# Third scan: the spreads of u and delta on 32-row tiles of the TensorE array, two quarters at a time

## The chip, the cores and the metric

The kernel runs on one core of one Trainium2 chip. The time is device microseconds of that core, the median of three executions; lower is better. A profile is one execution of its own, with its own time.

## What is computed

The reference is a chain of four layers on a tensor of 8 x 64 x 32 x 32: window attention with an MLP, an anti-aliased activation, a selective scan of eight tokens (`scan2` in the kernel) and a selective scan over whole pictures (`scan3`, the third scan of the title), each with norms and projections around it. The change lies in scan3 alone. Cut to what matters:

```python
dt = softplus(dtr @ dt_w.T + dt_b)          # delta, one value per channel and token
A = -exp(A_log)
def step(h, inp):
    dt_t, B_t, C_t, x_t = inp
    dA = exp(dt_t[..., None] * A)           # decay, channels x 16 states
    h = dA * h + (dt_t * x_t)[..., None] * B_t[:, None, :]
    y = einsum('bds,bs->bd', h, C_t)
    return h, y
```

Here u stands for dt_t * x_t. The recurrence runs over 1024 tokens of each picture.

## The kernel before, in words

Channels stand on partitions and tokens on columns. A value of delta or u belongs to a channel, but the state has 16 values per channel, so delta and u have to be spread: each channel's row is copied onto 16 partitions. TensorE does this with a matmul by a matrix of zeros and ones (`selr`); selector 4q + g has its ones in rows 32q + 8g to 32q + 8g + 7 alone, that is inside quarter q of the 128 rows. So that float32 comes through exactly, each source is split into a high and a low part (`parts`, written by ScalarE and GpSimd), and a spread is two matmuls of 512 columns that add up in one PSUM bank.

The work is 64 steps. A step is one group of 8 channels out of each quarter, 512 tokens, and its four quarters q = 0 to 3 are handled one after the other with q % 2 picking one of two PSUM banks for delta (`ps_d`) and one of two for u (`ps_u`). Four steps share one block of 512 tokens; at each such group of four steps the new block's delta, u, B and C are prepared.

In one step of scan3 the engines do this:

- TensorE (in the order of `body`): spreads of u for q = 0, 1 (`inputs`), spread of delta q = 0 (`decays`), spread of B (`states(0)`), spread of delta q = 1, spreads of u q = 2, 3, spread of C (`states(1)`), spreads of delta q = 2, 3, and then `r_py`: four float32 matmuls on 128x32 tiles (tile positions (0, 32q)), which sum the products over the states. Once per group of four steps it also does L1481 (delta's projection) and L1485 (B and C).
- ScalarE: `r_decay` (L1595), the exponential of the spread delta, one instruction per quarter; copies of spread B and C out of PSUM (L1605); parts of the preparation.
- DVE (VectorE): `r_feed` (L1630), u times B, for two quarters; then `r_state` (L1643), the scan itself, for these two quarters; then the same for q = 2, 3. Once per group it folds y (L1659).
- POOL (GpSimd): `r_prod` (L1702), state times C, four per step, and once per group seven more operations: L1707 (low parts of B and C), L1675, L1677, L1680, L1685 (softplus), L1690 and L1693, and L1671.

Every engine runs its own program in order; semaphores tie them. The lags are written by hand: at step s TensorE spreads B and C of step s - 2, delta of s - 5, u of s - 6 and sums y of s - 7, while DVE and POOL work on s - 6. In each group's third step the spread of B waits for POOL's L1707 (`lo_bc`), which POOL does after the products of its second step. L1481 and L1485 write the same bank `ps_m` as the spreads of B and C, so states(0) waits for ScalarE's relu (L1562) or copy (L1568) in those steps. y waits for `multiplied`, the products of its step.

Of the kernel before, what the change touches and what calls it, by code (L numbers as in the profile page):

```python
# [16 lines left out]
P = 128  # L17
# [42 lines left out]
def wait(eng, sem, value):  # L60

    if isinstance(value, int) and value <= 0:
        return
    eng.wait_ge(sem, value)
# [767 lines left out]
UNROLL, PEEL = 8, 8  # L832
# [589 lines left out]
def scan3(nc, consts, xc, selr, ysel):  # L1422
# [4 lines left out]
    with ExitStack() as ctx:  # L1427
# [5 lines left out]
        parts = m.sb("r_parts", [P, 2, 3, 2, N], F32R)  # L1433
# [5 lines left out]
        ps_d, ps_u, feed = m.banks("r_pd", 2), m.banks("r_pu", 2), m.banks("r_feed", 2)  # L1439
# [6 lines left out]
        hi_d, hi_u, hi_bc, lo_d, lo_u, lo_bc = (m.sem("r_" + t) for t in ("hid", "hiu", "hibc", "lod", "lou", "lobc"))  # L1446
# [7 lines left out]
        DT, DU, BC = range(3)  # L1454
# [9 lines left out]
        def _(pe):  # L1464
# [5 lines left out]
            def spread(bank, sel, which, par):  # L1470
                for part in range(2):
                    mm = pe.matmul(bank[:], selr[:, sel * P:(sel + 1) * P], parts[:, par, which, part],  # L1472
                                   start=(part == 0), stop=(part == 1))
                return mm

            def body(s, u):
                par = u // 4
                gi = s - u % 4
# [8 lines left out]
                def decays(qs):  # L1487
                    p, v = s - LAG_D, u - LAG_D
                    if not live(p, STEPS):
                        return  # L1490
                    for q in qs:
                        if v % 4 == 0 and q == 0:
                            pe.wait_ge(lo_d, p + 4)
                        wait(pe, decayed, 4 * p + q - 1)
                        spread(ps_d[q % 2], 4 * q + v % 4, DT, v % UNROLL // 4).then_inc(d_ps, 1)

                def states(which):

# [15 lines left out]
                def inputs(qs, p, v):  # L1514
                    if not live(p, STEPS):
                        return
                    for q in qs:
                        if v % 4 == 0 and q == 0:
                            pe.wait_ge(lo_u, p + 4)
                        wait(pe, fed, 4 * p + q - 1)  # L1520
                        spread(ps_u[q % 2], 4 * q + v % 4, DU, v % UNROLL // 4).then_inc(u_rep, 1)

                inputs((0, 1), s - LAG_U, u - LAG_U)
                decays((0,))
                states(0)
                decays((1,))
                inputs((2, 3), s - LAG_U, u - LAG_U)
                states(1)
                decays((2,))
                decays((3,))  # L1530
                p, v = s - LAG_Y, u - LAG_Y
                if live(p, STEPS):
                    if v % 4 == 0:
# [11 lines left out]
        def _(act):  # L1545
# [6 lines left out]
            def body(s, u):  # L1552
# [35 lines left out]
                def decays(qs):  # L1588
                    p, v = s - LAG_D, u - LAG_D
                    if not live(p, STEPS):  # L1590
                        return
                    for q in qs:
                        act.wait_ge(d_ps, 4 * p + q + 1)
                        wait(act, scanned, 4 * (p - 2) + q + 1)
                        act.activation(decay[:, v % 2, q], ps_d[q % 2][:], ACT.Exp,  # L1595
                                       scale=aneg[:, v % 4:v % 4 + 1]).then_inc(decayed, 1)
# [20 lines left out]
        def _(dve):  # L1617
# [3 lines left out]
            def body(s, u):  # L1621
                p, v = s - LAG_U, u - LAG_U
                if live(p, STEPS):
                    b, g, lc = v % 2, v % 4, v % UNROLL // 4
                    def inflow(q):
                        dve.wait_ge(u_rep, 4 * p + q + 1)
                        if g == 0:
                            dve.wait_ge(b_copied, p + q + 1)
                        wait(dve, scanned, 4 * p + q - 1)
                        dve.tensor_tensor(feed[q % 2][:], ps_u[q % 2][:], bs[:, lc, q], ALU.mult).then_inc(fed, 1)  # L1630
# [165 lines left out]
```

## Time and profile before

| | us |
|---|---|
| median of 3 runs | 2071.08 |
| lowest and highest | 2064.47, 2071.54 |
| the profiled execution, its own time | 2069.05 |
| its span | 2067.3 |
| scan3 in it, first matmul to last product | about 1432 to 1961 |

The span is what the profiler saw between the first and the last instruction; 1.75 us lie around it. Busy shares are of the whole span. PE is TensorE's matmuls, PEld its weight loads, which overlap matmuls. The granted clock of TensorE is 1.00 at 2.4 GHz and 0.50 at 1.2 GHz. A bracket at the end of a timeline row tells how long the engine had been idle before it, and for whom it waited; an x8 at its form means eight instructions merged into one row.

### The profile page before, as it was taken

Reading aid. Unit: us, or ns where it says so; the run is one execution under the profiler, and the core shown is the slowest. Engines: PE = TensorE matmul, PEld = TensorE weight load, DVE = VectorE, ACT = ScalarE, POOL = GpSimd, SP = SyncE. Lnnn points to the kernel's source line nnn. Section 1 sums busy time; section 2 is a strip of 40 time slices with the busy share of each in tenths; the row PEclk is TensorE's granted clock in tenths of the full one; section 3 lists DMA queues with packets and bytes.
Section 4 is the critical chain, followed back from the end, with each engine's and each line's share of the span. In section 5 each row is a group of like instructions: output and inputs, shape, how many; then the busy total and the mean of one; then the engine's idle time right before and its main releaser. Section 6 shows DMA issues by size and latency. Waiting matters only on the chain. (4 is left out here: it accounts for less than half of the span.)

```text
span 2067.3 us, 30819 instructions
## 1 busy us (share of the span) xinstructions
PE 1656.4 (80%) x9846; PEld 982.2 (48%) x9846; DVE 1602.7 (78%) x1580; ACT 1122.0 (54%) x1825; POOL 1391.9 (67%) x897
## 2 busy tenths in 40 slices
PE   5888787996777777787877777667788898888787
PEld 2555445883444444444444444325454555555323
DVE  3788655555899999999999999642699999999954
ACT  3444484344555555555555555365666666666355
POOL 1666401003999999999999999501799999999701
PEclk8999998997999999999999999888899999999888
DMA  4000000000000000000000000000000000000001
GB/s 130 2 0 0 1 0 1 1 1 0 1 1 1 0 0 0 0 0 0 0 0 0 0 0 0 18 0 1 1 1 0 0 0 0 0 0 0 1 12 41
DMA packets 5004, 11.04 MB, mean 5 GB/s; under 512 B 1744, under 2 KB 2768, under 8 KB 4688
## 3 DMA queue, kind: packets, MB, share of 16 engines
q1 hardware_dynamic: 4944, 10.29, 1.7%
q8 instruction: 32, 0.52, 0.1%
q14 instruction: 28, 0.23, 0.0%
HBM read 8.19 MB, written 2.10 MB: 5 GB/s over the span
## 5 line engine op out<-in xcount | busy, mean ns | idle before, releaser
L1157 POOL TENSOR_TENSOR s_ahead<-s_ahead,s_back 128x1024 f32<-128x1024 f32 x128 | 305.2, 2384 | 44.3 <-DVE s_back L1140 41.3
L1702 POOL TENSOR_TENSOR r_prod<-r_state,r_cs 128x512 f32<-128x512 f32 x256 | 323.5, 1304 | 16.3 <-DVE r_state L1643 15.9
L1194 POOL TENSOR_TENSOR s_prod<-s_ahead,s_cs 128x1024 f32<-128x1024 f32 x128 | 304.7, 2381 | 6.8 <-POOL s_ahead L1157 4.3
L1137 DVE TENSOR_TENSOR_SCAN s_ahead<-s_fore,s_pfeed 128x1024 f32<-128x1024 f32 x128 | 292.4, 2284 | 6.7 <-ACT s_fore L1056 1.6
L1140 DVE TENSOR_TENSOR_SCAN s_back<-s_aft,s_pfeed 128x1024 f32<-128x1024 f32 x128 | 289.4, 2261 | 0.0
L1056 ACT ACTIVATE s_fore<-s_pd,s_aneg 128x896 f32<-128x896 f32 x128 | 129.8, 1014 | 265.0 <-PE s_pd L936 265.0
L936 PE MATMUL s_pu<-s_partsu,selr 128*128 128x512 f32 x512 | 174.0, 464 | 100.0 <-DVE s_pfeed L1120 99.8
L1630 DVE TENSOR_TENSOR r_feed<-r_pu,r_bs 128x512 f32<-128x512 f32 x256 | 164.5, 686 | 65.0 <-PE r_pu L1472 65.0
L1595 ACT ACTIVATE r_decay<-r_pd,r_aneg 128x512 f32<-128x512 f32 x256 | 168.2, 685 | 24.4 <-PE r_pd L1472 24.1
L936 PEld LDWEIGHTS s_pu<-s_partsu,selr 128*128 128x128 f32 x512 | 94.1, 197 | 175.1 <-DVE s_pfeed L1120 124.0
L1120 DVE TENSOR_TENSOR s_pfeed<-s_pu,s_bs 128x1024 f32<-128x1024 f32 x128 | 157.8, 1233 | 18.6 <-PE s_pu L936 5.5
L1472 PE MATMUL r_pu<-r_parts,selr 128*128 128x512 f32 x512 | 162.7, 440 | 5.7 <-DVE r_feed L1630 5.7
L1643 DVE TENSOR_TENSOR_SCAN r_state<-r_decay,r_carry,r_feed 128x512 f32<-128x512 f32 x128 | 156.2, 1261 | 0.0
L1472 PE MATMUL r_pd<-r_parts,selr 128*128 128x512 f32 x512 | 155.4, 407 | 0.0
L936 PE MATMUL s_pd<-s_partsd,selr 128*128 128x512 f32 x512 | 150.1, 418 | 0.0
L994 PE MATMUL s_py<-s_prod,ysel 128*32 128x128 f32 x2048 | 142.5, 408 | 8.7 <-POOL s_prod L1194 8.7
L1643 DVE TENSOR_TENSOR_SCAN r_state<-r_decay,r_feed 128x512 f32<-128x512 f32 x128 | 148.5, 1201 | 0.0
L1472 PE MATMUL r_pm<-r_parts,selr 128*128 128x512 f32 x256 | 93.0, 446 | 59.3 <-POOL r_parts L1707 45.9
L1061 ACT ACTIVATE s_aft<-s_pd,s_aneg 128x896 f32<-128x896 f32 x128 | 129.9, 1015 | 0.0
L1472 PEld LDWEIGHTS r_pu<-r_parts,selr 128*128 128x128 f32 x512 | 95.1, 195 | 72.0 <-issue 39.2
L936 PEld LDWEIGHTS s_pd<-s_partsd,selr 128*128 128x128 f32 x512 | 105.0, 205 | 25.0
L650 POOL TENSOR_TENSOR logit<-logit,top 128x512 f32<-128x512 f32 x64 | 66.7, 1042 | 70.6 <-DVE top L621 70.6
(249 smaller groups left out, 3339.7 us busy)
## 6 DMA issues: line engine op xcount, KB each, us to landing
x_act<-in_x_dram SPq DMA_DIRECT2D x8, 256.0 KB, 5.3
out_dram<-x_act SPq DMA_DIRECT2D x16, 128.0 KB, 2.3
k_scan<-in_pack_scan_dram SPq DMA_DIRECT2D x1, 1600.0 KB, 10.2
k_fir<-in_pack_fir_dram SPq DMA_DIRECT2D x1, 1600.0 KB, 13.6
k_ln<-in_pack_ln_dram SPq DMA_DIRECT2D x3, 131.0 KB, 2.7
k_mlp<-in_pack_mlp_dram SPq DMA_DIRECT2D x2, 194.0 KB, 4.8
k_l<-in_pack_l_dram SPq DMA_DIRECT2D x1, 386.0 KB, 6.7
k_attn<-in_pack_attn_dram SPq DMA_DIRECT2D x1, 358.0 KB, 6.8
```

Source lines behind the costliest of these rows:

```text
L936: mm = pe.matmul(bank, selr[:, sel * P:(sel + 1) * P], parts[:, part], start=(part == 0), stop=(part == 1))
L994: mm = pe.matmul(ps_y[quad * 32:(quad + 1) * 32, j * NPX:(j + 1) * NPX], ysel[:, (2 * odd + g) * 32:(2 * odd + g + 1) * 32], terms[:, 2 * ...
L1120: dve.tensor_tensor(feed[:], ps_u[:], bs[:, buf].rearrange("p i n -> p (i n)"), ALU.mult).then_inc(fed, 1)
L1137: dve.tensor_tensor_scan(ahead[:, b], f, feed[:], 0.0, ALU.mult, ALU.add).then_inc(ahead_done, 1)
L1140: dve.tensor_tensor_scan(back[:, b, ::-1], a[:, ::-1], feed[:, ::-1], 0.0, ALU.mult, ALU.add).then_inc(back_done, 1)
L1157: pool.tensor_tensor(ahead[:, b], ahead[:, b], back[:, b], ALU.add).then_inc(summed, 1)
L1194: pool.tensor_tensor(prod[:, b], ahead[:, b], cs[:, buf].rearrange("p i n -> p (i n)"), ALU.mult).then_inc(prod_done, 1)
L1472: mm = pe.matmul(bank[:], selr[:, sel * P:(sel + 1) * P], parts[:, par, which, part], start=(part == 0), stop=(part == 1))
L1595: act.activation(decay[:, v % 2, q], ps_d[q % 2][:], ACT.Exp, scale=aneg[:, v % 4:v % 4 + 1]).then_inc(decayed, 1)
L1630: dve.tensor_tensor(feed[q % 2][:], ps_u[q % 2][:], bs[:, lc, q], ALU.mult).then_inc(fed, 1)
L1643: dve.tensor_tensor_scan(state[:, b, q], decay[:, b, q], feed[q % 2][:], start, ALU.mult, ALU.add).then_inc(scanned, 1)
L1702: pool.tensor_tensor(prod[:, v % 2, q], state[:, v % 2, q], cs[:, v % UNROLL // 4, q], ALU.mult).then_inc(multiplied, 1)
```

## The change

For u and for delta, the two quarters of a pair (0 and 1, or 2 and 3) are now spread by one helper, `pair`. Each of its matmuls takes only the 32 rows of its quarter, of `selr` and of `parts`, with tile position (32q, 0), so it uses a 32 x 128 tile of the array. The order inside is high part of the one quarter, high part of the other, low part of the one, low part of the other. The semaphore is raised by 2 after the last matmul; ScalarE and DVE wait for the whole pair, and TensorE waits until both banks of the pair have been read. The order of the step on TensorE becomes u 0 and 1, delta 0 and 1, B, u 2 and 3, C, delta 2 and 3, y. The spreads of B and C still use the old `spread` on the whole array. The number of matmuls and of their columns stays.

```diff
--- before.py
+++ after.py
@@ -1473,6 +1473,15 @@
                                    start=(part == 0), stop=(part == 1))
                 return mm
 
+            def pair(banks, sel, qs, which, par):
+                for part in range(2):
+                    for q in qs:
+                        rows = slice(32 * q, 32 * q + 32)
+                        mm = pe.matmul(banks[q % 2][:], selr[rows, (4 * q + sel) * P:(4 * q + sel + 1) * P],
+                                       parts[rows, par, which, part], start=(part == 0), stop=(part == 1),
+                                       tile_position=(32 * q, 0))
+                return mm
+
             def body(s, u):
                 par = u // 4
                 gi = s - u % 4
@@ -1488,11 +1497,10 @@
                     p, v = s - LAG_D, u - LAG_D
                     if not live(p, STEPS):
                         return
-                    for q in qs:
-                        if v % 4 == 0 and q == 0:
-                            pe.wait_ge(lo_d, p + 4)
-                        wait(pe, decayed, 4 * p + q - 1)
-                        spread(ps_d[q % 2], 4 * q + v % 4, DT, v % UNROLL // 4).then_inc(d_ps, 1)
+                    if v % 4 == 0 and qs[0] == 0:
+                        pe.wait_ge(lo_d, p + 4)
+                    wait(pe, decayed, 4 * p + qs[1] - 1)
+                    pair(ps_d, v % 4, qs, DT, v % UNROLL // 4).then_inc(d_ps, 2)
 
                 def states(which):
 
@@ -1514,20 +1522,17 @@
                 def inputs(qs, p, v):
                     if not live(p, STEPS):
                         return
-                    for q in qs:
-                        if v % 4 == 0 and q == 0:
-                            pe.wait_ge(lo_u, p + 4)
-                        wait(pe, fed, 4 * p + q - 1)
-                        spread(ps_u[q % 2], 4 * q + v % 4, DU, v % UNROLL // 4).then_inc(u_rep, 1)
+                    if v % 4 == 0 and qs[0] == 0:
+                        pe.wait_ge(lo_u, p + 4)
+                    wait(pe, fed, 4 * p + qs[1] - 1)
+                    pair(ps_u, v % 4, qs, DU, v % UNROLL // 4).then_inc(u_rep, 2)
 
                 inputs((0, 1), s - LAG_U, u - LAG_U)
-                decays((0,))
+                decays((0, 1))
                 states(0)
-                decays((1,))
                 inputs((2, 3), s - LAG_U, u - LAG_U)
                 states(1)
-                decays((2,))
-                decays((3,))
+                decays((2, 3))
                 p, v = s - LAG_Y, u - LAG_Y
                 if live(p, STEPS):
                     if v % 4 == 0:
@@ -1590,7 +1595,7 @@
                     if not live(p, STEPS):
                         return
                     for q in qs:
-                        act.wait_ge(d_ps, 4 * p + q + 1)
+                        act.wait_ge(d_ps, 4 * p + q // 2 * 2 + 2)
                         wait(act, scanned, 4 * (p - 2) + q + 1)
                         act.activation(decay[:, v % 2, q], ps_d[q % 2][:], ACT.Exp,
                                        scale=aneg[:, v % 4:v % 4 + 1]).then_inc(decayed, 1)
@@ -1623,7 +1628,7 @@
                 if live(p, STEPS):
                     b, g, lc = v % 2, v % 4, v % UNROLL // 4
                     def inflow(q):
-                        dve.wait_ge(u_rep, 4 * p + q + 1)
+                        dve.wait_ge(u_rep, 4 * p + q // 2 * 2 + 2)
                         if g == 0:
                             dve.wait_ge(b_copied, p + q + 1)
                         wait(dve, scanned, 4 * p + q - 1)
```

## Rows read from the trace of the kernel before

**Rows 1.** The page of before: busy shares of the engines over the whole span.

```profile
PE 1656.4 (80%) x9846; PEld 982.2 (48%) x9846; DVE 1602.7 (78%) x1580; ACT 1122.0 (54%) x1825; POOL 1391.9 (67%) x897
```

**Rows 2.** The page of before: TensorE and its clock in 40 slices (tenths).

```profile
PE   5888787996777777787877777667788898888787
...
PEclk8999998997999999999999999888899999999888
```

**Rows 3.** Windows: busy us and clock between starts of L1675 (one to five groups).

```profile
core 0: us, PE busy (x) PEld busy (x) DVE busy (x) ACT busy (x) POOL busy (x), PEclk, DMA share, GB/s
1463.20:1497.06 33.86, 28.63 (x120) 17.55 (x120) 30.26 (x36) 23.29 (x44) 30.38 (x26) 1.00 0.00 1
1497.06:1651.39 154.33, 131.36 (x580) 78.23 (x580) 144.47 (x166) 96.31 (x173) 151.56 (x121) 1.00 0.00 0
1528.18:1558.86 30.68, 26.30 (x116) 15.69 (x116) 28.43 (x34) 19.65 (x37) 30.27 (x25) 1.00 0.00 0
1651.39:1746.08 94.69, 82.65 (x348) 50.59 (x348) 86.05 (x100) 59.05 (x107) 91.00 (x73) 0.95 0.00 0
1746.08:1776.98 30.90, 26.26 (x116) 15.62 (x116) 29.23 (x34) 19.00 (x33) 30.32 (x25) 0.98 0.00 0
1776.98:1872.82 95.84, 83.57 (x348) 51.38 (x348) 85.96 (x100) 59.08 (x107) 91.07 (x74) 0.93 0.00 0
1872.82:1903.71 30.89, 26.23 (x116) 15.62 (x116) 29.20 (x34) 19.00 (x33) 30.31 (x25) 1.00 0.00 0
```

**Rows 4.** Waits of POOL, then of DVE, from 1497.06 to 1903.71 us.

```profile
POOL r_prod L1702 <- DVE r_state L1643: 5.8, 9, 0.9
...
DVE r_feed L1630 <- PE r_pu L1472: 30.9, 36, 2.4
```

**Rows 5.** Timeline of PE: one step that waits for nothing (start us, us).

```profile
1719.18 1.06 PE L1537 MATMUL r_py<-r_prod,ysel 128*32 128x512 f32 x8
...
1722.61 1.09 PE L1472 MATMUL r_pu<-r_parts,selr 128*128 128x512 f32 x4
...
1723.55 0.63 PE L1472 MATMUL r_pm<-r_parts,selr 128*128 128x512 f32 x2
...
1725.04 1.07 PE L1537 MATMUL r_py<-r_prod,ysel 128*32 128x512 f32 x8
```

**Rows 6.** Timeline: POOL's L1707 and what follows, clock at its upper level.

```profile
1526.95 1.26 POOL L1707 TENSOR_TENSOR r_parts<-r_bcf,r_parts 128x512 fp32r<-128x512 f32 x1
...
1528.27 0.30 PEld L1472 LDWEIGHTS r_pm<-r_parts,selr 128*128 128x128 f32 x2 [3.58 <-POOL r_parts L1707]
...
1530.12 1.32 DVE L1630 TENSOR_TENSOR r_feed<-r_pu,r_bs 128x512 f32<-128x512 f32 x2 [1.12 <-PE r_pu L1472]
```

**Rows 7.** Timeline: the same place with the clock at its lower level.

```profile
1775.75 1.27 POOL L1707 TENSOR_TENSOR r_parts<-r_bcf,r_parts 128x512 fp32r<-128x512 f32 x1
...
1777.08 1.22 PE L1472 MATMUL r_pm<-r_parts,selr 128*128 128x512 f32 x2 [3.16 <-POOL r_parts L1707]
...
1780.20 0.70 DVE L1630 TENSOR_TENSOR r_feed<-r_pu,r_bs 128x512 f32<-128x512 f32 x1 [2.39 <-PE r_pu L1472]
```

**Rows 8.** Timeline of PE, then DVE: from ScalarE's relu to the next feed.

```profile
1793.55 0.72 PE L1472 MATMUL r_pm<-r_parts,selr 128*128 128x512 f32 x2 [1.11 <-ACT r_relu L1562]
...
1799.97 1.30 DVE L1630 TENSOR_TENSOR r_feed<-r_pu,r_bs 128x512 f32<-128x512 f32 x2 [1.20 <-PE r_pu L1472]
```

**Rows 9.** Timeline of POOL, then DVE: the last step of an undisturbed group.

```profile
1578.40 10.22 POOL L1702 TENSOR_TENSOR r_prod<-r_state,r_cs 128x512 f32<-128x512 f32 x8
...
1580.02 1.30 DVE L1630 TENSOR_TENSOR r_feed<-r_pu,r_bs 128x512 f32<-128x512 f32 x2 [0.32 <-PE r_pu L1472]
...
1584.76 2.44 DVE L1643 TENSOR_TENSOR_SCAN r_state<-r_decay,r_carry,r_feed 128x512 f32<-128x512 f32 x2
```

**Rows 10.** Timeline: POOL in the first group, then DVE near the end.

```profile
1489.95 2.54 POOL L1702 TENSOR_TENSOR r_prod<-r_state,r_cs 128x512 f32<-128x512 f32 x2 [1.39 <-DVE r_state L1643]
...
1923.80 1.30 DVE L1630 TENSOR_TENSOR r_feed<-r_pu,r_bs 128x512 f32<-128x512 f32 x2 [0.29 <-PE r_pu L1472]
```

## The prediction

> **What bounds the kernel now.** The change touches scan3 alone, so I asked first which engine sets its pace. The busy shares of the whole span name TensorE first (80%) [rows 1], but they mix four layers. So I cut scan3 into its groups of four steps, at the starts of POOL's L1675, and read windows [rows 3]: POOL is busy 30.3 us in every group, and a group lasts 30.7 to some 32 us. POOL's nearest rival DVE has 28.4 us in groups whose scans start from zero and 29.2 in those that start from a carry; TensorE about 26 to 28. POOL is the bound. The gaps between its instructions are hand-overs inside its own chain (L1677 to L1685), so I take the shortest group, 30.68 us, as the floor of a group. No edit here touches a POOL instruction.
>
> The 13 whole groups from 1497.06 to 1903.71 take 406.65 us. The floor is 13 x 30.68 = 398.84, so 7.8 us lie above it, and POOL's waits say what most of them are: 5.8 us for DVE's scans [rows 4]. DVE in turn waited 30.9 us for spreads of u, and for nearly nothing else [rows 4]. Most of that is harmless; what counts is the part by which DVE comes late to the last step of a group. In [rows 3] the seven groups with the clock at 0.98 to 1.00 (five in one window of 154.33, then 30.90 and 30.89) average 30.87 us. The six with it at 0.95 and 0.93 (two windows of 94.69 and 95.84 us, three groups each) average 31.76. So nearly all that can be won is in groups where TensorE's clock has dropped.
>
> Three places carry DVE's waits:
>
> (a) Behind L1707. The spread of B waits for it, and everything of TensorE's queue waits behind that, u 2 and 3 included. From L1707's end to the feed it takes 1.91 us at the upper clock [rows 6] and 3.18 at the lower [rows 7]. Before the first of these feeds lie six matmuls of 512 columns (B, delta 1, u 2).
>
> (b) From ScalarE's relu to the next step's feed: 6.42 us [rows 8], in which TensorE does 16 such matmuls, y and L1485. DVE waits 1.20 us at its end. This comes in the groups that start from zero.
>
> (c) Behind y, which waits for POOL: y of step p - 2 stands ahead of u 0 and 1 of step p. It leaves POOL almost nothing: the last two products of the eight start at about 1578.40 + 10.22 - 2.5 = 1586.1, and the first of the two scans from 1584.76 ends at about 1586.0 [rows 9].
>
> **The change, part by part.** Unhindered, TensorE issues a full-array matmul every 0.235 us (four in 0.94: 1722.61 to 1723.55), and a step from y to y takes 5.86 us [rows 5].
>
> Pairing. Sixteen of the 20 spread matmuls of a step go on 32-row tiles. The trace has no row tiles; its nearest rows are y's 128x32 column tiles: eight instructions in 1.06 us [rows 5], four tiles side by side. So the cost of four paired matmuls lies between 0.94 us (one after the other) and 0.47 (two by two), and not below, since a column needs its slot in each of two passes. I take 0.47: the neighbour along the other axis shares fully, the two quarters write different banks, and the loads don't stand in the way, since two loads take 0.30 us together [rows 6], so the second comes about 0.11 after the first. That saves 4 x 0.47 = 1.9 us of TensorE's step.
>
> Changes of tile shape. Before, a step has two: into y and out of it. Now B and C stand between paired spreads, which adds four. Price from [rows 5]: 5.86 - 20 x 0.235 - 4 x 0.235 (y's four passes) = 0.22 for two, so 0.11 each. The upper bound is an array that empties and then loads: a lone matmul takes 0.63 - 0.235 = 0.40 us instead of 0.235, and the loads' 0.19 are no longer hidden, 0.35 in all. Taken: 0.11, the only shape change the trace shows; 0.44 a step, with 1.4 as the far end. TensorE's free-running step falls from 5.9 to about 4.4 us.
>
> The Trainium skill speaks against this part: TensorEngine Tiling (Array Packing), section Key Properties, says that changing the tiling mode, not just the tile, drains TensorE. The trace shows 0.11 us for it; by a full drain the sum would go to its far end.
>
> Coarser waits. The feed of q = 0 now waits for the low part of q = 1: about 0.11 us later in (c) (the offset of a load). u 2 and 3 wait for both feeds; DVE then has 2.3 to 2.4 us of scans [rows 9] to cover a pair of 0.47 plus some 0.4 of latency: nothing. ScalarE's first exponential likewise. Delta 2 and 3 wait for ScalarE's exponential of q = 1, which stands behind the copy of B: about 0.3 us of TensorE's step, hidden under POOL.
>
> What it is worth at each place. (a): six slots become four, one shape change more: 1.91 to about 1.55, and at the lower clock, with slots twice as long, 3.18 to about 2.5. (b): 16 slots become 10, three shape changes more, and the C spread now waits for ScalarE's copy of B (about 0.3): 6 x 0.235 - 0.33 - 0.3 = 0.8 of the 1.20 us. (c): 0.1 later, against a margin of 0.1.
>
> The clock works against it. TensorE stood idle 3.16 us before the lower-clock case [rows 7]; it will stand about 1 us longer. So I let all 13 groups have their low stretch. Such a group takes 31.76 now; less 0.7 for (a), and in every second one 0.8 for (b), but not under the floor and with 0.1 for (c), it comes to about 31.0. 13 x 31.0 = 403.0: a gain of 3.6 us. With the clock as now, 4.3. Taken: 4.
>
> First group: 33.86 us, 3.2 above the floor [rows 3], with waits for DVE such as 1.39 us [rows 10]. It has (b) once, and the first feed comes 0.3 earlier: gain 1.1.
>
> End: from the feed at 1923.80 [rows 10] DVE runs without a pause to its last scan; that feed is released through y by POOL, as in (c). Gain 0.
>
> **Sum:** 2069.05 (the profiled execution's own time, 2067.3 of span and 1.75 around it) - 4.0 - 1.1 = 2064.0 us. That execution lies 2.0 below the median of 2071.08, but inside the runs (2064.47 to 2071.54), and the mean of these and it is 2069.0; so I forecast 2064 as it stands.
>
> **The rivals.**
>
> *TensorE gets out of the way entirely.* POOL runs at its floor: -7.8 for the 13 groups and -2.3 for the first one's waits: 2059.0. For it: TensorE's 1.4 us less a step. Against it: (c) is a loop through POOL, which a faster TensorE hardly shortens.
>
> *No overlap, or loads that block* (the other side). If the pairs run one after the other, TensorE's step grows to 5.86 + 0.44 = 6.3 us, at the far end 7.3, and each feed of q = 0 comes 0.47 later than now. In (c) only 0.1 of that is covered, so 0.37 in each of 14 groups; (a) and (b) grow by 0.1 to 0.35 for each shape change, 0.4 a group. 14 x 0.77 + 0.5 at the end = 11: 2080. With the far end of the shape change TensorE has 4 x 7.3 + 1.1 + some 3 of waits = 33.3 us a group and becomes the bound: 2100. It decides from the point where four paired matmuls take over about 0.6 us. For it: nothing in the trace shows row tiles; against it: y. One rule of the Trainium skill would bring it about: TensorE: Matmul & The Clock Gate, Part 3, The mechanism, says that a weight load overlaps matmuls in flight only if its row group differs, and the low part's load has the row group of the high part's matmul. The trace disagrees for the full array, where loads of about 0.19 us hide inside a pitch of 0.235. The same page's measured speedup for four row tiles, 3.07, speaks for the overlap.
>
> *The clock.* TensorE's busy share of a group falls from 0.86 to about 0.67 (26.3 - 7.5 + 1.8 of 31). In the four slices from 1292 to 1499 us, where TensorE is busy 6 to 7 tenths, the clock is at 8 tenths; in others with 7 tenths it is at 9 [rows 2]. At 1.2 GHz throughout, its step would take some 9 us, more than POOL's 7.7. If every group lost, on top of today's time, what the three from 1776.98 lose to the floor (95.84 / 3 - 30.68 = 1.3 at a clock of 0.93) [rows 3], that is 13 x 1.3 = 17: 2086. It decides from a granted clock of about 0.85 in a group.
>
> *It doesn't matter at all:* DVE's lateness comes from chains I take for covered, and the time stays: 2069.
>
> **How the numbers follow.** Forecast 2064 (2060 to 2068): 0.48. Floor reached, 2059: 0.14. No change, 2069: 0.12. No overlap or blocking loads, 2080: 0.18. Clock, 2086: 0.08. About 0.5%, 10 us, is what a measurement of this kernel can tell from no change. Faster by more, under 2060.7 from the median: most of the floor case, a little of the forecast's spread: 0.17. Slower, over 2081.4: half of the no-overlap case, the clock case, and some spread of runs: 0.20. The same: 0.63. The range leaves out the far ends (a drained array, half of the clock case) and below reaches past the floor by the spread of runs: 2055 to 2083.
>
> **What would show it.** In the profile after: four paired matmuls of u in about 0.5 us of TensorE's time (over 0.8 would mean no overlap); TensorE's step around 4.4 us between y and y; its wait for L1707 longer by 1 us, the feed behind it at 1.6 or 2.5 us; POOL's waits for DVE under 3 us; groups of 30.7 to 31.1. A group under 30.6 would mean that POOL's floor was read wrongly, and one over 32 with POOL waiting for DVE that the pairs or the clock cost more than they give.

## The result and the profile after

The changed kernel takes 2119.75 us (median of four, 2117.50 to 2165.84) against 2067.77 us before (2063.75 to 2071.54): the ratio is 1.0248, with a 95% interval from 1.0225 to 1.0270. It is slower by 52 us, where I had forecast 2064 us: 7 us under the median then shown, and 5 under the profiled execution. Its profiled execution took 2121.61 us, with a span of 2119.8. Some kernels with row tiles have a second, longer time, 48 to 60 us above the first and at a lower mean clock of the span (2165.84 at 0.856 here, the others at 0.873 to 0.878); ratios leave it out, and what brings it about is open.

The page after: busy shares, then TensorE and its clock in 40 slices, to be read against [rows 1, 2].

```profile
PE 1698.2 (80%) x9846; PEld 907.7 (43%) x9846; DVE 1605.3 (76%) x1580; ACT 1130.4 (53%) x1825; POOL 1389.5 (66%) x897
...
PE   5888778996778887888887786586988878888877
...
PEclk8999999998999999999999999795658687777589
```

As many matmuls as before, POOL and DVE as busy as before, and TensorE busy for 42 us more, though each pair was meant to halve its work. The clock row points at a reason: up to slice 27 it is that of before within a tenth, and in the slices of scan3 behind it is at 5 to 8 tenths where it had been at 8 and 9. Windows show it as in [rows 3]: the first group, the 13 groups that follow, and the end up to the last product; then the two halves of one group. POOL's L1675 is L1680 here.

```profile
core 0: us, PE busy (x) PEld busy (x) DVE busy (x) ACT busy (x) POOL busy (x), PEclk, DMA share, GB/s
1463.17:1505.40 42.23, 39.14 (x122) 15.40 (x122) 28.95 (x34) 24.21 (x44) 30.18 (x25) 0.50 0.00 1
1505.40:1951.24 445.84, 374.94 (x1508) 145.34 (x1508) 378.49 (x432) 258.92 (x454) 391.72 (x314) 0.74 0.00 0
1951.24:2014.92 63.68, 53.98 (x192) 20.85 (x192) 55.01 (x63) 23.73 (x41) 48.90 (x40) 0.50 0.00 1
1694.20:1711.30 17.10, 12.56 (x68) 4.92 (x66) 15.66 (x19) 12.49 (x23) 13.68 (x12) 1.00 0.00 0
1711.30:1728.40 17.10, 16.12 (x50) 6.05 (x50) 13.35 (x15) 7.29 (x12) 16.62 (x14) 0.51 0.00 0
```

Where the time lies: the first group takes 42.23 us (33.86 before), the 13 groups 445.84 (406.65), the end 63.68 (57.39; that window of before runs from 1903.71 to 1961.10). That is 8.4 + 39.2 + 6.3 = 53.9 us, and the rest of the span gives 1.4 back. A group lasts 34.3 us on average, and POOL is busy 30.1 us in it, as before: it is not slower, it waits. The last two rows show how a group goes: 17.1 us at 2.4 GHz, 17.1 us at 1.2 GHz. At the lower level TensorE is busy 94% of the time, at the upper one 73% (12.56 of 17.10).

Some of the longest waits of three engines in the 13 groups (total us, times, longest), for [rows 4]:

```profile
DVE r_feed L1635 <- PE r_pu L1480: 59.7, 39, 3.5
...
PEld r_pm L1472 <- ACT r_bs L1610: 41.5, 52, 1.4
PE r_pm L1472 <- POOL r_parts L1712: 41.2, 13, 3.7
...
POOL r_prod L1707 <- DVE r_state L1648: 34.2, 39, 3.1
```

POOL waits 34.2 us for DVE's scans, up from 5.8, DVE 59.7 us for spreads of u, up from 30.9. The chain runs from TensorE to DVE to POOL. Now the timeline of PE through the low half:

```profile
1712.28 1.22 PE L1472 MATMUL r_pm<-r_parts,selr 128*128 128x512 f32 x2 [3.00 <-POOL r_parts L1712]
1713.43 1.22 PE L1480 MATMUL r_pu<-r_parts,selr 32*128 32x512 f32 x4
1714.57 1.22 PE L1472 MATMUL r_pm<-r_parts,selr 128*128 128x512 f32 x2
...
1716.87 1.94 PE L1542 MATMUL r_py<-r_prod,ysel 128*32 128x512 f32 x8
1718.74 1.22 PE L1480 MATMUL r_pu<-r_parts,selr 32*128 32x512 f32 x4
1719.76 1.05 PE L1480 MATMUL r_pd<-r_parts,selr 32*128 32x512 f32 x4
1720.74 1.22 PE L1472 MATMUL r_pm<-r_parts,selr 128*128 128x512 f32 x2
1721.89 1.22 PE L1480 MATMUL r_pu<-r_parts,selr 32*128 32x512 f32 x4
1723.04 1.22 PE L1472 MATMUL r_pm<-r_parts,selr 128*128 128x512 f32 x2
1724.19 1.22 PE L1480 MATMUL r_pd<-r_parts,selr 32*128 32x512 f32 x4
1725.34 1.94 PE L1542 MATMUL r_py<-r_prod,ysel 128*32 128x512 f32 x8
```

Three things stand in it. **The pairing works:** four paired matmuls on 32-row tiles last as long as two on the whole array (1.22 each), and the eight of u and delta take 1720.74 - 1718.74 = 2.00 us. **The shape changes are dear** (a change is the time between whole-array and 32-row matmuls beyond their slots, a slot being the step from one 512-column matmul to the next): two whole-array matmuls and a change take 1721.89 - 1720.74 = 1.15, and eight paired ones and a change 2.00; with x for a slot and c for a change, 2x + c = 1.15 and 4x + c = 2.00 give x = 0.425 and c = 0.30 us. **The step:** from y to y 8.47 us without a wait, where POOL's products and preparation want about 7.6. At this clock TensorE is the bound. (An estimate for the old step at this clock, from this slot and the 1.87 us from y to the next matmul: 20 x 0.425 + 1.87 = 10.4 us. So at this clock, too, the new step is shorter than the old one; what costs is how long the clock stays there.)

At the upper clock, PE then DVE, out of two places of the trace:

```profile
1705.72 0.73 PE L1472 MATMUL r_pm<-r_parts,selr 128*128 128x512 f32 x2 [0.92 <-ACT r_bs L1610]
...
1706.38 0.73 PE L1480 MATMUL r_pd<-r_parts,selr 32*128 32x512 f32 x4
...
1707.04 1.06 PE L1542 MATMUL r_py<-r_prod,ysel 128*32 128x512 f32 x8
...
1729.60 1.30 DVE L1635 TENSOR_TENSOR r_feed<-r_pu,r_bs 128x512 f32<-128x512 f32 x2 [2.32 <-PE r_pu L1480]
```

Two whole-array slots and a change take 0.66 us; less 2 x 0.235 from [rows 5] that is 0.19 for a change. Four paired matmuls and a change take 0.66 as well, so the four take 0.47. And TensorE had waited 0.92 us for ScalarE's copy of B ahead of C, which the shorter queue no longer covers. The last row is what a low half leaves: a feed that comes 2.32 us late though the clock is up again.

### The profile page after: what moved, and what is told of

Read it like the earlier page. It is cut to its first block and busy times, and to the rows that moved or that the text cites. A ratio compares the mean times of both kernels' runs of the same rounds, so it can differ in the third digit from the quotient of the medians.

```text
span 2119.8 us, 30644 instructions
## 1 busy us (share of the span) xinstructions
PE 1698.2 (80%) x9846; PEld 907.7 (43%) x9846; DVE 1605.3 (76%) x1580; ACT 1130.4 (53%) x1825; POOL 1389.5 (66%) x897
## 5 line engine op out<-in xcount | busy, mean ns | idle before, releaser
L1707 POOL TENSOR_TENSOR r_prod<-r_state,r_cs 128x512 f32<-128x512 f32 x256 | 320.5, 1280 | 55.0 <-DVE r_state L1648 52.3
L1472 PE MATMUL r_pm<-r_parts,selr 128*128 128x512 f32 x256 | 131.6, 607 | 73.2 <-POOL r_parts L1712 47.7
L1480 PE MATMUL r_pu<-r_parts,selr 32*128 32x512 f32 x512 | 125.4, 576 | 12.7 <-DVE r_feed L1635 12.5
L1480 PE MATMUL r_pd<-r_parts,selr 32*128 32x512 f32 x512 | 117.6, 545 | 2.4 <-ACT r_decay L1600 2.4
L1472 PEld LDWEIGHTS r_pm<-r_parts,selr 128*128 128x128 f32 x256 | 53.9, 262 | 144.5 <-POOL r_parts L1712 55.7
```

Of the source, the lines that this page charges most:

```text
L1480: mm = pe.matmul(banks[q % 2][:], selr[rows, (4 * q + sel) * P:(4 * q + sel + 1) * P], parts[rows, par, which, part], start=(part == 0), s ...
L1707: pool.tensor_tensor(prod[:, v % 2, q], state[:, v % 2, q], cs[:, v % UNROLL // 4, q], ALU.mult).then_inc(multiplied, 1)
```

## The experiments

The theory after this reading: the 32-row form lowers the granted clock, and most of the loss is that. The rivals: the new order and the coarser waits; the added changes of shape; the saved microseconds of work, that is, a less busy TensorE in whatever form. Below, "groups" is the mean of the whole groups after the first, "clock" the granted one and "busy" TensorE's share in them.

**The order and the waits alone, whole array.** The changed kernel with this edit to `pair`:

```diff
-                        rows = slice(32 * q, 32 * q + 32)
-                        mm = pe.matmul(banks[q % 2][:], selr[rows, (4 * q + sel) * P:(4 * q + sel + 1) * P],
-                                       parts[rows, par, which, part], start=(part == 0), stop=(part == 1),
-                                       tile_position=(32 * q, 0))
+                        mm = pe.matmul(banks[q % 2][:], selr[:, (4 * q + sel) * P:(4 * q + sel + 1) * P],
+                                       parts[:, par, which, part], start=(part == 0), stop=(part == 1))
```

> The changed kernel with the new order and the waits for whole pairs, but with matmuls on the whole array again. Clock theory (the shorter and narrower work lets the clock fall, and the fallen clock makes DVE late): TensorE is as busy as before, the granted clock of scan3 is about 0.96, and the time is that of before, 0 to +5 us. Rival (the order and the coarser waits cost it): most of the +52 us stays, over +25 us, with the clock near 0.95.

2079.48 us, ratio 1.0062 [1.0039, 1.0085]; groups 31.7 us, clock 0.96, busy 0.88. So all but 0.6% of the 2.5% hangs on the form of the matmuls. In this profile the first group takes 36.91 us at a clock of 0.94, 3 us more than before.

**The tile form alone, old order and old waits.** The kernel before, whose spreads of u and delta call this in place of `spread`:

```diff
+            def tile(bank, sel, which, par):
+                rows = slice(32 * (sel // 4), 32 * (sel // 4) + 32)
+                for part in range(2):
+                    mm = pe.matmul(bank[:], selr[rows, sel * P:(sel + 1) * P], parts[rows, par, which, part],
+                                   start=(part == 0), stop=(part == 1), tile_position=(32 * (sel // 4), 0))
+                return mm
```

> The kernel before with only the form of the spreads of u and delta changed: each quarter's two matmuls take a 32-row tile, in the old order and with the old waits. Two of one quarter can't overlap; quarters that stand next to each other in the queue can. Clock theory: the clock of scan3 falls to 0.8 or less although TensorE has nearly as much to do as before, and the time is +25 to +80 us. Rival (it is the new order that brings the low clock, by leaving TensorE idle in long pieces): the clock stays above 0.9 and the time within +15 us.

One run took 2116.67 us and three 2165.04 to 2167.37. The profile is of one of the three (2166.8): clock 0.66 over 12 groups of 37.6 us. The run to compare is the one of 2116.67, with a mean clock of the span of 0.880, against the changed kernel's 2117.50 to 2121.61 with 0.873 to 0.878. So the form brings the low clock without the new order, the high-then-low issue or the coarse waits, and in the one run that can be compared, which has no profile, it brings the whole loss. Neighbouring quarters overlap in this order too: four matmuls of u take 1.22 us at the lower clock, as in the changed kernel.

**B and C on row tiles too**, so that no shape changes are added. The changed kernel with this for states:

```diff
-                    spread(ps_m, 16 + 2 * (v % 4) + which, BC, v % UNROLL // 4).then_inc((b_rep, c_rep)[which], 1)
+                    rows = slice(32 * (v % 4), 32 * (v % 4) + 32)
+                    for part in range(2):
+                        mm = pe.matmul(ps_m[:], selr[rows, (16 + 2 * (v % 4) + which) * P:(17 + 2 * (v % 4) + which) * P],
+                                       parts[rows, v % UNROLL // 4, BC, part], start=(part == 0), stop=(part == 1),
+                                       tile_position=(32 * (v % 4), 0))
+                    mm.then_inc((b_rep, c_rep)[which], 1)
```

> The changed kernel with the spreads of B and C on 32-row tiles as well, so that the four extra changes of tile shape in a step are gone; everything else stays. Clock theory: no gain, +45 to +70 us against before, granted clock of scan3 at 0.75 or less. Rival (the changes of shape cost it, some 0.3 us each, 16 in a group): the time falls by 15 us or more against the changed kernel, to +35 or less.

2113.14 us, 1.0222 [1.0204, 1.0241]: 0.3% back of 2.5. Groups 34.1 us, and the clock lower still, 0.60. The four added shape changes are not the main cause; with fewer whole-array matmuls in the step the clock fell further, so the 0.3% may be what is left of two opposite effects, and is not the price of the changes.

**Whole-array fillers in the changed kernel.** Matmuls of a constant into the bank of B, overwritten by the spread after them: 12 in the step that waits for POOL's low parts of B and C, ahead of that wait and behind a wait for `bcf_done`, 4 ahead of B in the others and 2 ahead of each C.

```diff
+            def filler(n):
+                for _ in range(n):
+                    pe.matmul(ps_m[:], selr[:, 0:P], selr[:, 0:N], start=True, stop=True)
...
-                        if v % 4 == 0:
-                            pe.wait_ge(lo_bc, p + 4)
...
+                        if v % 4 == 0:
+                            pe.wait_ge(bcf_done, p + 4)
+                        filler(12 if v % 4 == 0 else 4)
+                        if v % 4 == 0:
+                            pe.wait_ge(lo_bc, p + 4)
                     else:
                         pe.wait_ge(b_copied, p + 1)
+                        filler(2)
```

> The changed kernel with added matmuls on the whole array whose result is overwritten: 4 (12 where POOL's low parts of B are awaited, ahead of that wait) before each spread of B and 2 before each spread of C. They add about 1.4 us of work to each of TensorE's steps at the upper clock. Clock theory: the clock of scan3 is over 0.95 and the time comes back to that of before or better, -10 to +8 us. Rival (shape changes or coarser waits): the time stays at +50 us or grows by the added work.

2083.66 us, 1.0077 [1.0053, 1.0100]. More work on TensorE and 35 us less time ((1.0248 - 1.0077) x 2068). Windows over the first group, the 13 groups and the end; columns as in [rows 3], here and for the next two kernels:

```profile
1462.97:1505.68 42.71, 39.44 (x168) 20.56 (x168) 30.60 (x36) 24.13 (x44) 30.40 (x25) 0.84 0.00 1
1505.68:1917.44 411.76, 386.90 (x1924) 188.26 (x1924) 374.87 (x430) 261.12 (x453) 392.55 (x314) 0.99 0.00 0
1917.44:1974.76 57.32, 42.11 (x212) 18.25 (x212) 54.52 (x63) 23.28 (x41) 48.94 (x40) 0.80 0.00 1
```

The groups give 34.1 us back and the end 6.4 (it is at the 57.39 of before); the first group stays as long as in the changed kernel, though its clock rose from 0.50 to 0.84.

**Busy on tiles.** Is it the idle time that the fillers fill, or their form? The changed kernel with each pair issued twice over, on its tiles (the second time gives the same values):

```diff
-                for part in range(2):
+                for part in (0, 1, 0, 1):
```

> The changed kernel with the matmuls of every pair issued twice, the first set overwritten: TensorE is about as long at work as before the change, but on 32-row tiles. If being at work for a shorter time is what lets the clock fall, the clock is over 0.9 and the time within +20 us of before. If the work on 32-row tiles does not hold the clock however long it lasts, the clock stays at 0.75 or less and the time rises above the changed kernel's, +60 to +130 us.

2295.84 us, 1.1116 [1.1083, 1.1149]. The profile is of its slowest execution (2355.2); the span's clock was 0.802 in it and 0.822 to 0.829 in the four others, against 0.939 to 0.944 with whole-array fillers. The window is of 11 groups.

```profile
1519.32:2068.10 548.78, 536.75 (x1992) 259.01 (x1990) 325.91 (x367) 222.15 (x384) 333.04 (x265) 0.55 0.00 0
```

TensorE is busy 98% and has a clock of 0.55; with whole-array fillers it was busy 94% and had 0.99. The busy share alone does not account for the clock.

**64-row tiles, old order.** The kernel before with `tile` as above, but on halves of the rows:

```diff
-                rows = slice(32 * (sel // 4), 32 * (sel // 4) + 32)
+                rows = slice(64 * (sel // 8), 64 * (sel // 8) + 64)
...
-                                   start=(part == 0), stop=(part == 1), tile_position=(32 * (sel // 4), 0))
+                                   start=(part == 0), stop=(part == 1), tile_position=(64 * (sel // 8), 0))
```

> As the run with tiles in the old order (+48 or +97 us, clock 0.66 over 13 groups), but each spread of u and delta takes a 64-row tile; changes of shape, order and waits are the same. If the number of rows at work decides about the clock, it lies well above 0.66, over 0.8, and the time at +5 to +35 us. If every tiled form is treated alike, or the changes of shape are the cost, it is as slow as with 32 rows, +45 us or more.

2215.51 us, 1.0706 [1.0688, 1.0723]. It is the second branch of the expectation that came, for the clock and for the time. The window is of 11 groups.

```profile
1502.53:1956.55 454.02, 430.20 (x1276) 201.47 (x1276) 326.39 (x364) 225.46 (x383) 332.75 (x265) 0.66 0.00 0
```

Clock 0.66 with TensorE busy 95%. Quarters 0 and 1 lie in the same half here, and so do 2 and 3, and neighbours do not overlap: at the upper clock the four matmuls of delta 2 and 3 and the change after them take 1.10 us (1615.13 to 1616.23). So there is more work than with 32 rows at a clock as low, and a group takes 41.3 us.

**The coarse waits of u alone**, whole array, order of before:

```diff
-                    for q in qs:
-                        if v % 4 == 0 and q == 0:
-                            pe.wait_ge(lo_u, p + 4)
-                        wait(pe, fed, 4 * p + q - 1)
-                        spread(ps_u[q % 2], 4 * q + v % 4, DU, v % UNROLL // 4).then_inc(u_rep, 1)
+                    if v % 4 == 0 and qs[0] == 0:
+                        pe.wait_ge(lo_u, p + 4)
+                    wait(pe, fed, 4 * p + qs[1] - 1)
+                    for part in range(2):
+                        for q in qs:
+                            mm = pe.matmul(ps_u[q % 2][:], selr[:, (4 * q + v % 4) * P:(4 * q + v % 4 + 1) * P],
+                                           parts[:, v % UNROLL // 4, DU, part], start=(part == 0), stop=(part == 1))
+                    mm.then_inc(u_rep, 2)
...
-                        dve.wait_ge(u_rep, 4 * p + q + 1)
+                        dve.wait_ge(u_rep, 4 * p + q // 2 * 2 + 2)
```

> The kernel before with the old order and the whole array, but the spreads of u issued two quarters together (high parts, then low parts) with one wait and one release for the pair. The new order with all coarse waits cost +12.8 us. If the coarser waits for u are most of that, +6 to +12 us here (the feed of quarter 0 then waits for two matmuls more, 0.47 us, 14 groups); if the order and delta's part are, 0 to +5 us.

2082.72 us, 1.0061 [1.0045, 1.0078], groups 32.1 us, clock 0.96: as much as the order-and-waits run lost. The mechanism is in the timeline, PE then DVE, at the place of [rows 9]:

```profile
1577.77 1.06 PE L1540 MATMUL r_py<-r_prod,ysel 128*32 128x512 f32 x8 [0.38 <-POOL r_prod L1705]
...
1580.94 1.30 DVE L1633 TENSOR_TENSOR r_feed<-r_pu,r_bs 128x512 f32<-128x512 f32 x2 [0.31 <-PE r_pu L1522]
```

From y to the feed 3.17 us; before it was 2.71 (1577.31 to 1580.02): 0.46 more, the two slots of q = 1, in a loop through POOL that had 0.1 to spare. POOL's waits for DVE rise to 16.2 us. On the tiles, where q = 1 runs beside q = 0, the same stretch of the filler kernel, from its y at 1674.70, is this:

```profile
1675.70 1.12 PE L1494 MATMUL r_pm<-y_inner,r_wdtb 128*128 x2
1676.75 0.74 PE L1480 MATMUL r_pu<-r_parts,selr 32*128 32x512 f32 x4
1677.61 1.30 DVE L1643 TENSOR_TENSOR r_feed<-r_pu,r_bs 128x512 f32<-128x512 f32 x2 [1.01 <-PE r_pu L1480]
```

It takes 2.91 us, 0.20 more than before. That is not the coarse wait: L1494, on the whole array, now stands ahead of a 32-row pair, and a change of shape is 0.19. From the pair's start to the feed it is 0.86 us, and 0.86 too in the last kernel of this section, which waits for each quarter by itself (1647.50 to 1648.36).

**The new order alone**, whole array, old waits: the kernel before with

```diff
-                decays((0,))
+                decays((0, 1))
                 states(0)
-                decays((1,))
                 inputs((2, 3), s - LAG_U, u - LAG_U)
                 states(1)
-                decays((2,))
-                decays((3,))
+                decays((2, 3))
```

> The kernel before with the new order of the step (delta of quarters 0 and 1 ahead of B, delta 2 and 3 last), the whole array, and the old waits for single quarters. If the order is most of the 12.8 us of the earlier run, +6 to +12 us; if the coarser waits are, 0 to +5 us.

2065.09 us, 0.9985 [0.9973, 0.9996] over 12 runs; groups 30.9, clock 0.98. POOL waits 0.9 us for DVE in all (5.8 before). The order is the one part of the change that helps, by 3 us, just clear of the noise.

**Fillers in the kernel before**, 12 of them at the wait for the low parts of B and C, none elsewhere (`filler` and the moved waits as above):

```diff
+                        filler(12 if v % 4 == 0 else 0)
+                        if v % 4 == 0:
+                            pe.wait_ge(lo_bc, p + 4)
```

> The kernel before with 12 matmuls on the whole array, whose result is overwritten, ahead of the wait for POOL's low parts of B, once in four steps (2.8 us of work in a wait of 3.2 us). If the low stretches of the clock in six of thirteen groups are what costs the kernel before its time over POOL's floor, the clock of scan3 is 1.00 in nearly all groups and the time falls by 3 to 8 us. Rival (the fillers hold up the spread of B and what stands behind it): 0 to +8 us.

2065.59 us, 0.9981 [0.9971, 0.9992]; groups 30.9 us, clock 1.00. **New order and these fillers together:**

> The kernel before (whole array, old waits) with the new order of the step and the 12 fillers ahead of the wait for POOL's low parts of B. Each alone gave -3 to -4 us, and each by taking DVE's lateness out of the same place, the end of a group. If they take the same microseconds, -3 to -6 us together; if they add up, -7 to -9 us. Groups of 30.8 us, clock 1.00.

2066.45 us, 0.9987 [0.9973, 1.0001]; groups 30.9, clock 1.00. The two gains don't add. In each, POOL's waits for DVE are all but gone (5.8 us before), so it seems that both take away the same waits, and what is left is POOL. In windows over 13 groups, fillers first, the order second:

```profile
1499.04:1900.35 401.31, 377.19 (x1664) 232.77 (x1664) 374.94 (x430) 251.18 (x453) 394.37 (x314) 1.00 0.00 0
```

```profile
1497.32:1898.79 401.47, 346.63 (x1508) 207.13 (x1508) 375.43 (x430) 253.07 (x453) 393.60 (x313) 0.98 0.00 0
```

**Fillers in the changed kernel at that wait alone** (12, and none elsewhere):

> The changed kernel with the 12 whole-array fillers ahead of the wait for POOL's low parts of B alone, and none elsewhere (the run with fillers everywhere gave a clock of 0.99 over 13 groups and +16 us). If the clock falls because of the long wait, it stays above 0.95 and the time is +5 to +18 us. If it falls because the rest of the step, too, has little whole-array work, the clock lies between 0.75 and 0.9 and the time at +25 to +45 us.

2128.91 us, 1.0288 [1.0273, 1.0302]: slower than the changed kernel without them, against what I expected. PE and POOL in the timeline:

```profile
1709.73 3.01 PE L1487 MATMUL r_pm<-selr 128*128 128x512 f32 x12
1709.88 1.29 POOL L1720 TENSOR_TENSOR r_parts<-r_bcf,r_parts 128x512 fp32r<-128x512 f32 x1
...
1712.58 0.63 PE L1472 MATMUL r_pm<-r_parts,selr 128*128 128x512 f32 x2
```

The low parts are there at 1711.17, but B starts at 1712.58: after a low half TensorE comes to this place late, and the fillers no longer lie in idle time. A filler pays where the queue waits anyway, and there it didn't. The clock rose to 0.79 only, inside the range that I had put beside the second branch (too little whole-array work in the rest of the step); the time went past both of my ranges. In this trace the clock falls again at 1722 us, with no wait of TensorE over 1.49 us since 1712.58. So the long wait is not the only place where it falls.

**The best I could make of the tiles**: the kernel with fillers, and the waits fine again. `pair` waits for and releases each quarter by itself, and ScalarE and DVE wait as before:

```diff
+                        if part == 0:
+                            wait(pe, free, 4 * p + q - 1)
...
+                        if part == 1:
+                            mm.then_inc(done, 1)
...
-                        act.wait_ge(d_ps, 4 * p + q // 2 * 2 + 2)
+                        act.wait_ge(d_ps, 4 * p + q + 1)
...
-                        dve.wait_ge(u_rep, 4 * p + q // 2 * 2 + 2)
+                        dve.wait_ge(u_rep, 4 * p + q + 1)
```

> The changed kernel with the fillers everywhere (clock held, +16 us) and single waits and releases for each quarter instead of one for the pair. With the whole array the coarse wait for u cost 0.47 us a feed and +13 us. On tiles a pair takes 0.47 us in all, so if the wait costs only the offset of the second quarter, 0.1 to 0.2 us, the time falls by no more than 5 us, to +11 to +16. If the coarse wait is what keeps the +16, it falls by 8 us or more.

2079.31 us, 1.0050 [1.0031, 1.0069]; groups 31.4, clock 1.00, first group 38.8 us at 0.96. It is still slower than before. Its profile is of the fastest of its four runs (2075.07). What remains in it is in the first group (4.9 us over before), where the fillers' own time can lie on the path, and in the groups (408.06 against 406.65 us, where the three kernels with POOL's waits taken away have 401). TensorE's loads for u wait 0.7 us for DVE's feeds in the groups, against 6.2 with the coarse waits: what the fine ones save is the wait for banks.

The loss of 0.0248 x 2068 = 51 us, by these runs: holding the clock gives 35 back, and more if the fillers cost time themselves. Of the 16 left (0.0077 x 2068), the two profiles (of before and with fillers) put 8.9 in the first group (42.71 against 33.86) and 5.1 in the 13 groups. Finer waits take away about half of that in the profiles, 3.9 and 3.7 us; by the ratios it is 6, but their intervals overlap. What remains is 10 over the kernel before, and the order hides a gain of 3 in it. Candidates are the changes of shape (0.19 us each at the upper clock, 0.19 of them in the loop through POOL), the fillers themselves, and round trips to ScalarE that lost their cover. I have no run that parts these.

## Why the prediction was wrong, point by point

**The bound, and where the time could be won: right.** POOL's busy time per group didn't move (30.1 against 30.3 us), and no kernel's groups average less than 30.86 us, which the three kernels that take away POOL's waits reach (the floor was put at 30.68). The prize was 8 to 10 us at most.

**The pairs: right.** 0.47 us for four, the lower of my bounds, as four took the time of two on the whole array (1.22 us at the lower clock, 0.73 at the upper). In the pair at 1708.03 all four weight loads, two for each row group, are done 0.30 us after its start, with its first matmuls still running. The Trainium skill's rule in TensorE: Matmul & The Clock Gate, Part 3, The mechanism, that a load overlaps matmuls in flight only if its row group differs, is not what this trace shows.

**The changes of shape: mis-sized.** Taken 0.11, measured 0.19 us at the upper clock and 0.30 at the lower, six a step instead of two, and one more that I left out, behind L1481 or L1485, in the two steps of a group that have them. The 0.11 came from the changes into and out of y, whose tiles use all 128 rows, and shared a remainder of 0.22 between two; 0.35 was my far end, so it is inside the bounds. The difference, 0.08 us for each of six changes in four steps, is some 2 us of TensorE's time a group, and at a held clock TensorE is not the bound. The Trainium skill's sentence in TensorEngine Tiling (Array Packing), Key Properties, that a change of the tiling mode drains TensorE, is nearer to this trace than my choice was: a lone matmul takes 0.40 us instead of 0.235, and 0.19 us is about that difference.

**The coarse waits: right for the tiles, by the rows that can be compared.** I took 0.11 us for the feed of q = 0 in (c), and from pair to feed the coarse wait cost nothing (0.86 us either way). The feed still came 0.20 later, by the change of shape that I had left out, in the place where I had said that nothing was to spare. On the whole array the same waits cost 0.46 us a feed and 12.6 us of time. For u 2 and 3 and delta 2 and 3 I took the wait for both banks as free; the fine waits took 5.5 us of waiting for feeds from TensorE, and no run shows what that alone was worth.

**The step of TensorE: 4.4 us was foretold.** At the upper clock the trace's stretches add up to 1.00 (y) + 1.13 (u and delta, 4 x 0.235 + 0.19) + 4 x 0.66 = 4.8 us; it never runs so, since ScalarE's copies hold it up. The one place where I let that cost anything had 0.3 us; the wait for the copy of B is 0.92 in the row above, and TensorE's loads wait 41.5 us for it over the 13 groups, against 8.8 before.

**The clock: the step that failed.** The sum let all 13 groups have a low stretch and priced such a group as one of before, at 31.76 us, to come down to 31.0 by the change's gains; measured were 34.3 us, at a clock of 0.74. I had the mechanism among the rivals, at a chance of 0.08 and a price of 17 us; the fillers give 35 back. Three errors in it:
- I measured the danger by TensorE's busy share, 0.86 falling to 0.67, and set it against slices of the profile with that share and a clock of 0.8. At the upper clock it did fall, to 0.73 (12.56 / 17.10); over the 13 groups it is 0.84 (374.94 / 445.84), as in [rows 3] (131.36 / 154.33 = 0.85), because the same work lasts longer at the lower clock, and the clock is 0.74 where [rows 3] had 1.00. And 98% busy on tiles had 0.55. The slices that I compared with hold no row tiles, and their busy share did not carry over.
- I priced it by what the groups of before lose at a clock of 0.93. But in those groups the low stretches were short. At 1.2 GHz a step takes 8.47 us (I had written "some 9", and the condition with it), more than POOL's, so TensorE becomes the bound for half of each group, and the chain TensorE, DVE, POOL carries it into the upper half (2.32 us at 1729.60).
- I took the wait for L1707 to be what drops the clock, and let it grow by 1 us. It hardly grew (PE waited 41.2 us in the 13 groups, against 39.8 before; 3.00 at 1712.28, 3.16 in [rows 7]), and the clock stayed low for 17.1 us. In the kernel before it was back after about 7, as windows of 2 us behind [rows 7] show (columns as in [rows 3]); in between TensorE was as busy as in the changed kernel:

```profile
1775.00:1777.00 2.00, 0.00 (x0) 0.00 (x0) 2.00 (x3) 0.00 (x0) 2.00 (x3) 0.71 0.00 0
1777.00:1779.00 2.00, 1.92 (x5) 1.54 (x6) 0.81 (x1) 0.60 (x1) 1.85 (x3) 0.50 0.00 0
1779.00:1781.00 2.00, 2.00 (x6) 1.60 (x5) 0.70 (x1) 0.69 (x1) 1.87 (x2) 0.50 0.00 0
1781.00:1783.00 2.00, 2.00 (x6) 1.32 (x4) 1.95 (x3) 1.00 (x2) 1.87 (x3) 0.59 0.00 0
1783.00:1785.00 2.00, 2.00 (x13) 0.97 (x13) 1.67 (x3) 1.61 (x4) 2.00 (x2) 1.00 0.00 0
```

This is the longest of the six low stretches in the 13 groups of before; the other five were half as long. In the changed kernel all 13 groups have one, of 17 us or more. So the clock falls twice as often and takes some 2.5 to 5 times as long to come back: the tiles delay its return more than they bring about its fall.

For the first group I took a gain of 1.1 us and for the end 0; they lost 8.4 and 6.3, at a clock of 0.50 in both. The end's loss is the clock's: the fillers gave it back whole. The first group's is not settled. In the whole-array run of the order and the waits it took 36.91 us at a clock of 0.94, and with the order alone 33.85, so some 3 of the 8.4 are what the coarse waits cost there; with fillers it took 42.71 us at a clock of 0.84.

**The signs I had named** did their work: "one over 32 with POOL waiting for DVE" is what the profile shows, and both causes I had written beside it, pairs or clock, were then parted by the fillers and the whole-array run. The sign for the wait for L1707, longer by 1 us, did not come, and a step of 4.4 us was never seen.

## What to carry to other kernels

Row tiles halve TensorE's slots, but in a kernel whose bound is another engine the saved slots are worth next to nothing, while the clock they ran at can be lost: read the granted clock of the stretch first, and work out the step at 1.2 GHz against the step of the engine that bounds. If that step is the longer one, the tile form is a risk that the saving has to pay for, the more so the longer the clock stays low. When two quarters are handed over together, look at what the first one then waits for: two slots of the other on the whole array (0.46 us a feed), nothing where both run side by side. And look at the order of the queue by itself, since here the plain reordering, on the whole array, was the part that gained, if only 3 us.

## What was unexpected of the hardware

- The form of the matmuls went with the clock, and how busy TensorE was did not: 0.55 at 98% busy (32-row tiles twice, in the slowest execution), 0.66 at 95% (64-row tiles), 0.74 at 84% (the change), 0.60 at 87% (B and C on tiles too), against 0.98 at 86% (new order, whole array) and 0.99 at 94% (the change with whole-array fillers).
- The Trainium skill, TensorE: Matmul & The Clock Gate, Part 1, ties the clock to how busy TensorE has been. If busy is read as the share in these rows, this case's runs disagree for row tiles: 98% busy, and 0.55.
- A change between the whole array and 32-row tiles costs 0.19 us at 2.4 GHz and 0.30 at 1.2 GHz.
- Row tiles overlap also where high and low part of one quarter stand next to each other (the old order): four matmuls of u last 1.22 us at the lower clock in both, so the interleaving in the change was not needed for that.
